# Attention 2's row maxima taken from PSUM three banks at a time in two sets, in place of two banks at a time in three sets

## The chip, the cores and the metric

The kernel runs on one core of one Trainium2 chip. The metric is the device time of one execution in microseconds (us), median of three runs. Below, PE is TensorE (PEld its weight loads), DVE is VectorE, ACT is ScalarE, POOL is GpSimd, SP is SyncE, and SPq is SP's issuing of DMAs.

## What is computed

For each of 16 batches, 512 query rows of 256 channels attend twice to a context of 1601 rows, with a Mamba-2 block between. Attention 2, which the change touches, has 8 heads of 32 channels:

```python
x = _L0_xattn_ref(x, ctx, ctx, mask, ...)          # attention 1, 16 heads of 16, layernorm
h = _mamba2_block(x, ...)
# attention 2
q = (_ln(h, ln_w, ln_b) @ Wq).reshape(b, Lq, 8, 32)
k = (enc @ Wk).reshape(b, Lk, 8, 32)
scores = einsum('bqhd,bkhd->bhqk', q, k) * 1/sqrt(32)
p = softmax(where(pad_mask, -1e9, scores), axis=-1)  # needs the maximum of each row of scores
out = h + (einsum('bhqk,bkhd->bqhd', p, v).reshape(b, Lq, D) @ Wo)
```

## The kernel before

One loop runs over the 16 batches, and each engine has its own program in it, written out by hand and tied to the others by semaphores. An engine executes its program in order, so whatever an engine waits for holds up all that stands behind it.

**The raw stage.** The softmax is taken on transposed scores (keys on the partitions), so each row's maximum has to be known first, as an extra row of the stacked queries. For that, attention 2's scores are computed once more with the queries on the partitions. This stage stands between the Mamba block and attention 2's scoring groups. It works on 2 groups of 4 heads; a group has 4 heads x 4 query tiles x 4 key chunks of 402 columns, 64 products, and each fills one PSUM bank. `entry1` on PE writes the products of an entry into a set of banks (L991), `entry1` on DVE reduces the set to one maximum per product with one instruction (L1642), and frees it. Before the change an entry has 2 products, there are 32 entries in a group, and three sets (banks 0 and 1, 2 and 3, 4 and 5): PE may fill entry n once DVE has freed entry n - 3 (L984). After a group's last entry `maxima1` on DVE folds the four chunk maxima of each row (L1622) and splits the negated maxima in two parts (L1625, L1627). One entry, "turn", stands after the first four entries of group 1: PE transposes the maxima of group 0 into a set (L987), and DVE copies them to a row (L1637). That makes 65 entries (`NENT1`).

**Forward projections.** Between entries PE also projects the first six items of the next batch (`FRONT`: two of queries, 512 columns, four of keys, about 402 columns each, four matmul passes an item, L933), one after every seventh entry (`FRONT_EVERY = 7`, L1319): after entries 6, 13, 20, 27, 34 and 41. They use banks 6 and 7. ACT takes each item out of PSUM in two instructions (`take`, L1372 and L1375), POOL splits it in parts with three instructions (`parts`, L737, L740, L743), with two pieces of the next mask converted after each item (L712). When the last item's parts are done, SP issues `stack(b + 1, 0)` (L655 to L657): 13 transfers inside SBUF that build the stacked keys `KS[0]` and queries `QS[0]` of the next batch's attention 1 (L550, L553, L556). Behind them in SP's program stand the loads of `maskt`.

**What comes after the stage.** PE waits until all entries are freed (L1323), and goes on with attention 2's first scoring group: `scores` (L1010), `times_v` (L1035), and beside them, slot by slot, raw entries of the next batch's attention 1 (`entry`, L971, from `CUTS`, L429). The very first slot has entry 0, which waits for all 13 transfers of `stack(b + 1, 0)` (L954).

```python
def forward():  ...  project(b + 1, front.pop(0), ...)
for n in range(NENT1):
    entry1(b, n)
    if n % FRONT_EVERY == FRONT_EVERY - 1 and front:
        forward()
```

Of the kernel before, what the change touches and what calls it, by code (L numbers as in the profile page):

```python
# [22 lines left out]
ALU = mybir.AluOpType  # L23
ACT = mybir.ActivationFunctionType
AX = mybir.AxisListType
# [4 lines left out]
GH = 4  # L30
# [15 lines left out]
MROW1 = KROWS1 + NPART  # L46
# [5 lines left out]
def xattn_mamba(nc, x, xt, ctxt, mask, maskt, mask1, wq0, bq0, wk0, bk0, wv0, bv0, wo0, bo0, ln_g, ln_b,  # L52
# [4 lines left out]
    QT = T // P  # L57
# [6 lines left out]
    CW = -(-SE // (2 * NCHUNK)) * 2  # L64
# [6 lines left out]
    RAW = GH * QT * NC  # L71
    NENT = G0 * (RAW + 1) + NC + 1
    NCOUNT = G0 * (RAW + 1)
    UNITS = GH * QT * NC // 2
    NENT1 = G1 * UNITS + 1
    NPJ0 = DT + NC + NC + KT
    NPJ = 2 * NPJ0
# [12 lines left out]
    with ExitStack() as ctx:  # L90
# [144 lines left out]

        top = max(top_attention, place[0])
        assert top <= nc.sbuf_usable_end, (top, nc.sbuf_usable_end)

        mask1_s = PR[:, :, :, :].rearrange("p a h t -> p (a h t)").bitcast(U8)[:, 0:S]

# [207 lines left out]
        ENTRIES1 = [("raw", 0, k) for k in range(UNITS)]  # L448
        ENTRIES1 += [("raw", 1, k) for k in range(4)] + [("turn", 0, 0)]
        ENTRIES1 += [("raw", 1, k) for k in range(4, UNITS)]  # L450
        NSETS = 3
        assert len(ENTRIES1) == NENT1

        def raw1_place(k):
            h, i, c = k // (QT * NC // 2), k // (NC // 2) % QT, k % (NC // 2)
            return h, i, c, (PAIRED[2 * c], PAIRED[2 * c + 1])

        OUT_BANK = [5, 7, 6, 3]
        XT1_BANK = [2, 4]
# [442 lines left out]
        def _(pe):  # L902
# [71 lines left out]
            def entry1(b, n):  # L974

                kind, g, k = ENTRIES1[n]
                bank = 2 * (n % NSETS)
                if kind == "raw" and k == 0:
                    for half in range(2):
                        pe.wait_ge(s_k1[g][half], LEAD + (b + 1) * STACK1)  # L980
                    pe.wait_ge(s_k1pad, G1 * (b + 2))
                    pe.wait_ge(s_qs1[g], LEAD + (b + 1) * STACKQ1)
                if n >= NSETS:
                    pe.wait_ge(s_r1free, LEAD + b * NENT1 + n - NSETS + 1)  # L984
                if kind == "turn":
                    pe.wait_ge(s_nm1, b * G1 + g + 1)
                    pe.transpose(ps[0:NPART1 * 16, bank, 0:P], f(nm1[:, :]), ident[:, :]).then_inc(s_r1, 1)  # L987
                    return
                h, i, _, cc = raw1_place(k)
                for e in range(2):  # L990
                    mm = pe.matmul(ps[:, bank + e, 0:CW], QS1[g][0:MROW1 + 1, h, i * P:(i + 1) * P],  # L991
                                   KS1[g][0:MROW1 + 1, h, cc[e]:cc[e] + CW], start=True, stop=True)
                mm.then_inc(s_r1, 1)

            def scores(b, gi, t, between):
# [529 lines left out]
        def _(dve):  # L1525
# [92 lines left out]
            def maxima1(b, g, n):  # L1618

                m = b * G1 + g  # L1620
                dve.wait_ge(s_r1free, LEAD + b * NENT1 + n + 1)
                nc.vector.tensor_reduce(mxr[:, :], mx[:, :, :].rearrange("p c n -> p n c"), AX.X, ALU.max)\  # L1622
                    .then_inc(s_mx1, 1)
                dve.wait_ge(s_mx1, 2 * m + 1)
                nc.vector.tensor_scalar(nm1[:, 0:16], mxr[:, :], -1.0, None, ALU.mult).then_inc(s_mx1, 1)  # L1625
                dve.wait_ge(s_mx1, 2 * m + 2)
                nc.vector.scalar_tensor_tensor(out=nm1[:, 16:32], in0=mxr[:, :], scalar=-1.0, in1=f(nm1[:, 0:16]),  # L1627
                                               op0=ALU.mult, op1=ALU.subtract).then_inc(s_nm1, 1)

            def entry1(b, n):  # L1630

                kind, g, k = ENTRIES1[n]
                bank = 2 * (n % NSETS)
                dve.wait_ge(s_r1, b * NENT1 + n + 1)
                if kind == "turn":
                    dve.wait_ge(s_mload1[1], LEAD + b * 16 * NPART1)
# [1 line left out]
                    dve.wait_ge(s_mrow1, b * G1 + g + 1)  # L1638
                    nc.vector.memset(small[:, 1:2], 0.0).then_inc(s_r1free, 1)
                    return  # L1640
                h, i, c, _ = raw1_place(k)
                nc.vector.tensor_reduce(mx[:, 2 * c:2 * c + 2, h * QT + i], ps[:, bank:bank + 2, 0:CW], AX.X, ALU.max)\  # L1642
                    .then_inc(s_r1free, 1)
                if k == UNITS - 1:
                    maxima1(b, g, n)
# [275 lines left out]
```

## Time and profile before

| | us |
|---|---|
| median of 3 runs | 8576.49 (8573.46 to 8576.82) |
| the profiled execution | 8574.72 |
| its span, first to last instruction | 8572.7 |
| PE busy | 7618.3 (89%) |
| DVE busy | 5016.2 (59%) |
| ACT busy | 3401.1 (40%) |
| POOL busy | 1911.0 (22%) |

A batch takes some 522 us, of which the raw stage is about 63. In the rows of a timeline the columns are start, duration of the merged run of instructions (both us), engine, line, operation, tiles, count, and in brackets the idle time of that engine before it with what ended it. In a table of stretches each engine has its busy us and its count of instructions; PEclk is the clock granted to TensorE (1.00 is 2.4 GHz, 0.50 is 1.2 GHz), DMA the busy share of the 16 DMA engines.

### The profile page before, as it was taken

What the parts mean: (1) busy time and instruction counts of PE and PEld (TensorE: products, weight loads), DVE (VectorE), ACT (ScalarE), POOL (GpSimd) and SP (SyncE); (2) the same over time, 40 slices, a digit from 0 to 9 for tenths busy, and PEclk for the clock granted to TensorE, in tenths of its full rate; (3) what the DMA queues carried; (4) which work ended last, traced back from release to release, by engine and by line L of the source; (5) the groups of instructions that cost most, each with busy time, mean ns of one, the idle gap of its engine ahead of it and who ended that gap; (6) DMA issues with size and microseconds to landing.
All of it is one profiled execution on the core that took longest, in us unless ns stands there. A gap on an engine that the chain in (4) does not pass through costs nothing.

```text
span 8572.7 us, 128046 instructions
## 1 busy us (share of the span) xinstructions
PE 7618.3 (89%) x37252; PEld 3425.4 (40%) x37572; DVE 5016.2 (59%) x12397; ACT 3401.1 (40%) x4278; POOL 1911.0 (22%) x1864
## 2 busy tenths in 40 slices
PE   3989899898998989989899898989989899898998
PEld 0343433434344343433534334343443434335343
DVE  3566465664656556565664656646566565656656
ACT  0424435343352434535244352443524345252443
POOL 3040130402203031130401304022040311304113
PEclk6989989899998989989899898999989999898998
DMA  3142230423314133231422304233141332314223
GB/s 72 27 80 38 41 67 11 80 38 51 58 22 75 30 62 56 36 54 29 77 41 36 66 16 80 38 49 60 20 77 30 59 58 34 56 30 73 45 36 62
DMA packets 230652, 422.16 MB, mean 49 GB/s; under 512 B 37209, under 2 KB 128251, under 8 KB 229769
## 3 DMA queue, kind: packets, MB, share of 16 engines
q1 hardware_dynamic: 227927, 413.21, 28.3%
q8 instruction: 351, 5.75, 0.3%
q14 instruction: 326, 2.67, 0.1%
q10 hardware_dynamic: 2048, 0.53, 0.0%
HBM read 191.17 MB, written 8.54 MB: 23 GB/s over the span
## 4 chain that ended last, share of the span: by engine, by line
PE 73%; DVE 10%; issue 8%; DMA 3%; ACT 3%; SPq 2%; POOL 1%; DVEq 0%; ACTq 0%; POOLq 0%
PE ps L1035 13%; PE ps L971 11%; PE ps L1006 8%; PE ps L933 8%; PE ps L1008 7%; DVE mx L1642 5%; PE ps L1010 4%; PE ps L1040 4%; PE ps L991 2%; PE ps L1191 2%; PE ps L1154 2%; PE ps L1245 1%; DMA qst<-q1hl 1%; PE ps L1273 1%; PE ps L1106 1%
## 5 line engine op out<-in xcount | busy, mean ns | idle before, releaser
L1413 ACT ACTIVATE PR<-ps 128x1024 f32<-128x1024 f32 x2496 | 2498.3, 1023 | 2514.8 <-PE ps L1008 1395.2
L1613 DVE CUSTOM_DVE_ANT_0 ps<-ps,maskq 128x402 f32<-128x402 f32 x4203 | 2408.7, 587 | 1517.2 <-PE ps L971 1374.8
L1035 PE MATMUL ps<-PR,vbuf 128*32 128x512 f32 x9984 | 1346.9, 612 | 5.1 <-ACT PR L1413 5.1
L1008 PE MATMUL ps<-maskk,identb 128*128 128x512 bf16 x3008 | 1142.8, 380 | 0.0
L971 PE MATMUL ps<-kst,qst 96*128 96x402 bf16 (+1 forms) x3115 | 1017.9, 340 | 97.0 <-DVE mx L1613 67.8
L1642 DVE TENSOR_REDUCE mx<-ps 128x2 f32<-128x804 f32 x1024 | 933.6, 985 | 197.6 <-PE ps L991 195.6
L991 PE MATMUL ps<-kst,qst 100*128 100x402 f32 x2048 | 751.5, 494 | 257.9 <-DMA qst<-q1hl 155.2
L1006 PE MATMUL ps<-qst,kst 99*128 99x512 bf16 x2496 | 950.9, 381 | 7.3
L1010 PE MATMUL ps<-qst,kst 102*128 102x512 f32 x1664 | 768.0, 526 | 100.1 <-ACT PR L1413 70.7
L971 PEld LDWEIGHTS ps<-kst,qst 96*128 96x128 bf16 x3115 | 282.1, 97 | 1183.9 <-DVE mx L1613 817.5
L751 POOL MEMSET kst<- 96x252 f32 (+1 forms) x34 | 8.7, 255 | 3061.8 <-PE ps L1035 3015.4
L991 PEld LDWEIGHTS ps<-kst,qst 100*128 100x128 f32 x2048 | 416.7, 241 | 571.5 <-DVE mx L1642 381.9
L1613 DVE DVE_READ_ACCUMULATOR2_ANT mx<- 128x1 f32 x4203 | 591.6, 141 | 0.0
L1651 DVE RECIPROCAL rsm<-ps 128x128 f32<-128x128 f32 x80 | 76.6, 957 | 866.3 <-PE ps L1059 866.3
L712 POOL TENSOR_SCALAR maskk<-stage 128x512 bf16<-128x512 int32 (+1 forms) x238 | 428.3, 1800 | 336.6 <-DMA stage<-in_maskt 328.6
L971 PE MATMUL ps<-KS,QS 96*128 96x402 bf16 x1088 | 410.8, 378 | 102.9 <-DVE mx L1613 74.1
L712 POOL TENSOR_SCALAR maskq<-stage 128x402 bf16<-128x402 int32 (+1 forms) x272 | 427.4, 1571 | 301.7 <-DMA stage<-in_mask 278.9
L933 PE MATMUL ps<-ctxs,wk_s 128*128 128x402 f32 (+1 forms) x1056 | 468.5, 571 | 24.0 <-ACT rest L1375 23.1
L1040 PE MATMUL ps<-PR,ones 128*32 128x512 f32 x3328 | 447.8, 610 | 0.0
L1008 PEld LDWEIGHTS ps<-maskk,identb 128*128 128x128 bf16 x3328 | 327.3, 98 | 265.4 <-issue 1.3
L1010 PEld LDWEIGHTS ps<-qst,kst 102*128 102x128 f32 x1664 | 330.1, 206 | 244.5 <-ACT PR L1413 151.0
L1006 PEld LDWEIGHTS ps<-qst,kst 99*128 99x128 bf16 x2496 | 243.9, 98 | 410.2 <-ACT PR L1413 183.9
(197 smaller groups left out, 7899.2 us busy)
## 6 DMA issues: line engine op xcount, KB each, us to landing
kst<-khl SPq DMA_DIRECT2D x300, 200.1 KB, 7.7
stage<-in_maskt SPq DMA_DIRECT2D x204, 256.0 KB
stage<-in_mask SPq DMA_DIRECT2D x204, 201.0 KB
kst<-khl SPq DMA_DIRECT2D x96, 402.0 KB, 8.6
kst<-khl SPq DMA_DIRECT2D x96, 398.5 KB, 11.6
ctxs<-in_ctxt SPq DMA_DIRECT2D x17, 1601.0 KB, 17.7
qst<-q1hl SPq DMA_DIRECT2D x96, 256.0 KB
win_s<-in_w_in SPq DMA_DIRECT2D x16, 1288.0 KB, 5.7
```

The costliest lines, as they stand in the source:

```text
L712: nc.gpsimd.tensor_scalar(dst, stage[0:rows, n % 2, 0:w], 0.0, MASKED, ALU.is_equal, ALU.mult)\
L933: mm = pe.matmul(o, l, r, start=(k == 0), stop=(k == DT - 1))
L971: pe.matmul(ps[:, bank, 0:w], QS[gi][0:KROWS, h, i * P:(i + 1) * P], KS[gi][0:KROWS, h, c0:c0 + w], start=True, stop=True).then_inc(s_raw, 1)
L991: mm = pe.matmul(ps[:, bank + e, 0:CW], QS1[g][0:MROW1 + 1, h, i * P:(i + 1) * P], KS1[g][0:MROW1 + 1, h, cc[e]:cc[e] + CW], start=True, s ...
L1006: pe.matmul(o, KS[gi][0:SROWS, h, t * P:(t + 1) * P], QS[gi][0:SROWS, h, :], start=True, stop=False)
L1008: mm = pe.matmul(o, identb[:, :], maskk[:, t, :], start=False, stop=True)
L1010: mm = pe.matmul(o, KS1[gi - G0][0:SROWS1, h, t * P:(t + 1) * P], QS1[gi - G0][0:SROWS1, h, :], start=True, stop=True)
L1035: mm = pe.matmul(ps[32 * j:32 * j + 32, 6, :], l, PR[:, t % 2, j, :], start=(t == 0), stop=(t == KT - 1), tile_position=(0, 32 * j))
L1040: mm = pe.matmul(ps[32 * j:32 * j + 32, 7, :], ones[:, 0:32], PR[:, t % 2, j, :], start=(t == 0), stop=(t == KT - 1), tile_position=(0, 32 ...
L1413: nc.scalar.activation(PR[:, t % 2, 2 * half:2 * half + 2, :], ps[:, 2 * half:2 * half + 2, :], ACT.Exp, scale=scale).then_inc(s_p, 1)
L1613: nc.vector.tensor_tensor_reduce(src, src, maskq[:, i, c0:c0 + w], 1.0, -3.0e38, ALU.add, ALU.max, mx[:, c, h * QT + i:h * QT + i + 1]).th ...
L1642: nc.vector.tensor_reduce(mx[:, 2 * c:2 * c + 2, h * QT + i], ps[:, bank:bank + 2, 0:CW], AX.X, ALU.max)\
```

## The change

An entry now has three products in place of two (`WIDE = 3`), so a group has 22 entries: 21 of three banks and one of a single bank, since 64 is 21 x 3 + 1. There are two sets (banks 0 to 2 and 3 to 5) in place of three: PE may fill entry n once DVE has freed entry n - 2. The stage has 45 entries in place of 65. The products are numbered through, so the maxima are stored in another order, and the reduction of `maxima1` reads them accordingly. The number of products, the columns of each, the turn after the first four entries of group 1, and `FRONT_EVERY` are as they were.

```diff
-    UNITS = GH * QT * NC // 2
+    WIDE = 3
+    UNITS = -(-GH * QT * NC // WIDE)
...
+        mx_flat = mx[:, :, :].rearrange("p c n -> p (c n)")
...
-        NSETS = 3
+        NSETS = 2
-        def raw1_place(k):
-            h, i, c = k // (QT * NC // 2), k // (NC // 2) % QT, k % (NC // 2)
-            return h, i, c, (PAIRED[2 * c], PAIRED[2 * c + 1])
+        def raw1_chunks(k):
+            return range(WIDE * k, min(WIDE * (k + 1), GH * QT * NC))
...
-                bank = 2 * (n % NSETS)
+                bank = WIDE * (n % NSETS)
...
-                h, i, _, cc = raw1_place(k)
-                for e in range(2):
+                for e, n in enumerate(raw1_chunks(k)):
+                    h, i, c = n // (QT * NC), n // NC % QT, n % NC
                     mm = pe.matmul(ps[:, bank + e, 0:CW], QS1[g][0:MROW1 + 1, h, i * P:(i + 1) * P],
-                                   KS1[g][0:MROW1 + 1, h, cc[e]:cc[e] + CW], start=True, stop=True)
+                                   KS1[g][0:MROW1 + 1, h, PAIRED[c]:PAIRED[c] + CW], start=True, stop=True)
...
-                nc.vector.tensor_reduce(mxr[:, :], mx[:, :, :].rearrange("p c n -> p n c"), AX.X, ALU.max)\
+                nc.vector.tensor_reduce(mxr[:, :], mx_flat.rearrange("p (n c) -> p n c", c=NC), AX.X, ALU.max)\
...
-                h, i, c, _ = raw1_place(k)
-                nc.vector.tensor_reduce(mx[:, 2 * c:2 * c + 2, h * QT + i], ps[:, bank:bank + 2, 0:CW], AX.X, ALU.max)\
+                done = raw1_chunks(k)
+                nc.vector.tensor_reduce(mx_flat[:, done[0]:done[-1] + 1], ps[:, bank:bank + len(done), 0:CW], AX.X, ALU.max)\
```

## Rows read from the trace of the kernel before

**Rows 1.** The page: the chain that ended last, by engine.

```profile
PE 73%; DVE 10%; issue 8%; DMA 3%; ACT 3%; SPq 2%; POOL 1%; DVEq 0%; ACTq 0%; POOLq 0%
```

**Rows 2.** Groups of instructions, whole run: count, busy us, mean ns, idle before, releaser.

```profile
L1642 DVE TENSOR_REDUCE mx<-ps 128x2 f32<-128x804 f32 x1024 | 933.6, 985 | 197.6 <-PE ps L991 195.6
...
L1559 DVE TENSOR_TENSOR vbuf<-ps,bv_s 128x256 f32<-128x256 f32 (+1 forms) x208 | 88.2, 424 | 43.0 <-PE ps L933 26.5
```

**Rows 3.** Timeline of DVE, first batch's raw stage.

```profile
551.29 6.41 DVE L1642 TENSOR_REDUCE mx<-ps 128x2 f32<-128x804 f32 x7 [9.07 <-PE ps L991]
559.80 12.92 DVE L1642 TENSOR_REDUCE mx<-ps 128x2 f32<-128x804 f32 x14 [2.10 <-PE ps L991]
573.78 10.01 DVE L1642 TENSOR_REDUCE mx<-ps 128x2 f32<-128x804 f32 x11 [1.06 <-PE ps L991]
583.82 0.26 DVE L1622 TENSOR_REDUCE mxr<-mx 128x16 f32<-128x64 f32 x1
584.42 2.79 DVE L1642 TENSOR_REDUCE mx<-ps 128x2 f32<-128x804 f32 x3
...
588.40 0.27 DVE L1637 CAST mrow_f<-ps 32x128 fp32r<-32x128 f32 x1
...
588.80 25.35 DVE L1642 TENSOR_REDUCE mx<-ps 128x2 f32<-128x804 f32 x28
```

**Rows 4.** Timeline of PE, same stage: fills alone.

```profile
550.21 2.38 PE L991 MATMUL ps<-kst,qst 100*128 100x402 f32 x6 [9.71 <-DMA qst<-q1hl]
...
588.54 0.99 PE L991 MATMUL ps<-kst,qst 100*128 100x402 f32 x4 [0.61 <-DVE mx L1642]
...
595.26 0.63 PE L991 MATMUL ps<-kst,qst 100*128 100x402 f32 x2 [0.26 <-DVE mx L1642]
```

**Rows 5.** Timeline of PE, same stage: four of the six forward projections.

```profile
555.88 3.51 PE L933 MATMUL ps<-ctxn,wq_s 128*128 128x512 f32 x4
...
564.02 1.88 PE L933 MATMUL ps<-ctxn,wq_s 128*128 128x512 f32 x4
...
584.68 2.40 PE L933 MATMUL ps<-ctxs,wk_s 128*128 128x402 f32 x4
...
591.23 1.49 PE L933 MATMUL ps<-ctxs,wk_s 128*128 128x395 f32 x4
```

**Rows 6.** Table of stretches by granted clock (columns: PE, PEld, DVE, ACT, POOL, PEclk, DMA).

```profile
549.00:559.10 10.10, 8.89 (x19) 5.52 (x19) 6.41 (x7) 0.00 (x0) 2.01 (x2) 0.50 0.80 108
559.20:569.40 10.20, 8.17 (x30) 4.82 (x29) 9.49 (x11) 2.53 (x4) 8.85 (x8) 1.00 0.29 80
569.50:572.80 3.30, 3.26 (x7) 1.84 (x6) 3.21 (x4) 0.00 (x0) 3.14 (x3) 0.50 0.02 4
572.90:583.00 10.10, 8.15 (x31) 4.74 (x29) 9.22 (x11) 2.17 (x4) 8.49 (x9) 1.00 0.30 82
583.20:586.40 3.20, 3.20 (x7) 2.01 (x7) 3.10 (x7) 0.00 (x0) 3.04 (x3) 0.50 0.03 6
586.60:596.60 10.00, 8.01 (x31) 4.69 (x29) 9.65 (x13) 2.15 (x4) 7.59 (x9) 1.00 0.29 79
596.80:614.00 17.20, 15.47 (x34) 8.53 (x34) 17.20 (x20) 0.00 (x0) 3.34 (x3) 0.50 0.89 129
```

**Rows 7.** Timelines of ACT, POOL and SPq behind the last forward projection.

```profile
592.76 0.59 ACT L1372 ACTIVATE khl<-ps,cols 128x395 bf16<-128x395 f32 x1 [4.56 <-PE ps L933]
...
594.38 0.88 POOL L737 TENSOR_TENSOR rest<-rest,khl 128x395 f32<-128x395 f32 x1
...
596.06 0.94 POOL L743 TENSOR_TENSOR khl<-rest,khl 128x395 bf16<-128x395 f32 x1
...
597.46 4.77 SPq L553 DMA_DIRECT2D KS<-khl  x6
602.28 5.32 SPq L556 DMA_DIRECT2D QS<-qhl  x6
```

**Rows 8.** Table of stretches at the stage's end, columns as in rows 6.

```profile
612.00:613.00 1.00, 0.53 (x2) 0.00 (x0) 1.00 (x2) 0.00 (x0) 0.00 (x0) 0.50 0.97 320
613.00:614.00 1.00, 0.00 (x0) 0.00 (x0) 1.00 (x2) 0.00 (x0) 0.00 (x0) 0.50 0.12 41
```

**Rows 9.** Timeline of PE at the start of the first scoring group.

```profile
614.37 0.79 PE L1010 MATMUL ps<-qst,kst 102*128 102x512 f32 x1 [1.84 <-DVE mx L1642]
614.96 0.56 PE L971 MATMUL ps<-KS,QS 96*128 96x402 bf16 x1
```

More of the change, by code:

```diff
@@ L1632, in entry1 @@
                 kind, g, k = ENTRIES1[n]
-                bank = 2 * (n % NSETS)
+                bank = WIDE * (n % NSETS)
                 dve.wait_ge(s_r1, b * NENT1 + n + 1)
```

## The prediction

> **What bounds the kernel now.** I read the chain of waits first. It is 73% PE and 10% DVE [rows 1]. The group of L1642 alone has 933.6 us of busy time in the whole run [rows 2], 58 us of each batch's raw stage of 63. So in this stage, and here only, DVE sets the pace. Its timeline shows that: after the turn it does 28 reductions in 25.35 us without an idle moment; less the 0.98 of the last that is 24.37 over 27 steps, 0.90 us each [rows 3]. In its first half it idles 2.10 and 1.06 us, both behind a forward projection on PE [rows 3, 5]. PE meanwhile does a pair of products in 0.63 us and then idles 0.26 [rows 4]. Second, I read the granted clock. It is 1.00 in three stretches of 10 us and 0.50 between them, and stays at 0.50 from 596.8 on, when PE has no more forward projections [rows 6]. Third, I followed what the forward projections are for, since the change shifts them: that chain ends at the transfers of `stack(b + 1, 0)` [rows 7 to 9], and it decides the forecast. I work on the first batch's stage; the other 15 are alike within 3 us. Times below count from PE's first product, at 550.2.
>
> **1. Fewer reductions (a gain).** A reduction of 804 columns takes 0.985 us [rows 2] and DVE starts one every 0.90. What 402 more columns cost is not in the trace. From 256 to 804 columns read from PSUM, in two different operations, 0.424 grows to 0.985 [rows 2], 1.02 ns a column, or 0.41 us for 402; half a step would be 0.45. I take 0.42, so a wide reduction lasts 1.40 and its step is 1.32, or 0.44 us a bank against 0.45. By steps, 42 x 1.32 + 2 x 0.48 = 56.4 us against 64 x 0.90 = 57.7: 1.3 us less in a stage, 21 us in all. With 0.45 for the third bank it is nothing (1.35 a step, 0.45 a bank), and with 0.41 it is 28 us. The fixed part by the rows is 0.90 - 0.84 = 0.06 us for each of the 20 reductions saved.
>
> The Trainium skill, "Perfetto Trace Analysis", section "Optimizing Scalar/DVE Operations", gives DVE about 125 ns of access overhead per operation on PSUM and says that grouping into larger operations improves throughput if the engine is saturated. By that figure the 20 reductions would be worth 2.5 us a stage, 40 us in all; the trace shows half of it. The same section says that breaking up instructions may let work be completed sooner where DVE causes bubbles on other engines, and that speaks against this change.
>
> **2. Two sets in place of three (a loss at the low clock).** With two sets, a set's cycle is its reduction plus its refill, and two cycles interleave. Refill of two banks at the high clock: 0.63 us; four banks 0.99, so 0.18 a bank and 0.81 for three. At the low clock six banks took 2.38 us [rows 4]; a bank is 402 columns at 1.2 GHz, 0.335, so three take 1.37. Some 0.05 us of handover lies on either side. High: 1.40 + 0.81 + 0.10 = 2.31 for two steps, under 2 x 1.32, so DVE stays the bound. Low: 1.40 + 1.37 + 0.10 = 2.87 against 2.64, 0.11 us lost an entry. Before, three sets had 2.7 us for 0.98 + 1.04 + 0.10, so nothing was lost. With 40 entries, half to all of them low: 2 to 4.5 us a stage; none if the clock stays high.
>
> **3. Less cover for a forward projection (a loss).** Count from the moment that a set comes free. High clock: PE's streams of three banks end after 0.05 + 0.10 + 0.55 = 0.70; a key item takes 1.34 (the last took 1.49 with its tail, [rows 5]); the next set is filled 0.76 later, at 2.8. DVE has the rest of one reduction (1.24) and one more (1.32), until 2.56: it idles 0.25. For a query item (1.71) 0.6. Low clock: streams end at 1.2, a key item takes 2.68, the next set is full at 5.1, and DVE ran out at 2.78: it idles 2.4; for a query item (3.41) 3.1. The same recipe for the kernel before gives 0 and 0.2 at high, 1.85 and 2.6 at low; the trace has 2.10 after the first (low, with the clock rising during it) and 1.06 after the third, which ran partly low [rows 3, 5, 6].
>
> **4. The projections meet the low clock.** Before, six projections are one in 7 x 0.90 = 6.3 us plus stalls. One that runs at the low clock is followed by 10 us of high clock, and the next one falls into it: the pattern of low, high, low, high [rows 5, 6]. After, they are 7 x 1.32 = 9.3 us apart plus 2 of stalls, so most of them start when the clock has fallen again. I count, for projections 1 to 5, idle times on DVE of 2.2 (low, clock rising), 3.1, then 1.2, 2.4 and 2.1: 11 us, against 3.4 for the same five before (2.10 and 1.06 by the trace, 0.2 by the recipe). Bounds: all at the high clock 2 x 0.6 + 3 x 0.25 = 2.0; all at the low one 2 x 3.1 + 3 x 2.4 = 13.4.
>
> **5. maxima1, the short entry, the turn.** `maxima1` takes DVE 0.6 (583.82 to 584.42 [rows 3]), as before, and covers the refill behind the one-bank entry at the high clock. The turn takes 0.4 (588.40 to 588.80), in which the set behind it can't be refilled in time: 0.6 (high) to 1.1 (low) us of idle.
>
> **6. When the last forward projection ends.** This is the term that matters. Before, it is the sixth of 65 entries' worth, after entry 41, and ends at 592.7, 42.5 us into the stage; 23 entries follow. After, entry 41 is one of 45, and three follow. First reduction starts at 1.4. Entries 0 to 39, which have to be reduced before entry 41 can be filled, are 38 wide ones, a short one and the turn: 38 x 1.32 + 0.48 + 0.6 + 0.4 = 51.7. Then 0.7 to 1.2 of filling and the item itself, 1.34 to 2.68, likely 2.3. With stalls of 11, bubbles of 2 and the turn's 1.1: 1.4 + 51.7 + 1.0 + 2.3 + 14.1 = 70.5. Since some of these stalls overlap a bubble already counted, I take 69.5. Bounds: all high 1.4 + 51.7 + 0.7 + 1.3 + 2.0 + 0.6 = 57.7; all low 1.4 + 51.7 + 1.2 + 2.7 + 13.4 + 1.1 + 4.4 = 75.9.
>
> **7. What hangs on it.** Behind the last item stand ACT (592.76), POOL (594.38 to 597.0), then twelve DMA issues on SP's queue from 597.46 to 607.6 [rows 7], and the transfers keep the DMA engines at 0.97 until 613, when the share drops to 0.12 [rows 8]. That is 20.3 us from the end of the item. Before, 20.7 us of reductions covered it, and the transfers landed 2 us before PE first needs them: L971 starts at 614.96, 64.8 us into the stage, released by the end of the stage, not by a DMA [rows 9]. After the change only three entries, 3 us, stand there. The chain is as long (0.5 shorter, as POOL will not be busy with a mask piece when the item comes), so L971 can start at 69.5 + 19.8 = 89.3, which is 24.5 us later than before. PE is in order, and L971 is its second matmul of the scoring group, so all of attention 2's scoring and the raw entries of the next batch beside it wait, about 14 us in which PE, ACT and DVE have nothing. The stage itself gets some 10 us longer, which ends inside this wait. The `maskt` loads behind the transfers shift with them and with the scoring group, and the two rows of maxima that ACT issues behind the last `take` come before the transfers land; both cost nothing more. PE starts the scoring group at the low clock as it does now.
>
> **Sum.** 16 x 24.5 = 392 us on a span of 8572.7. The profiled run took 8574.7 and the median is 8576.5, so I add it to the median: 8968, and say 8970. Bounds by step 6: all high 57.7 + 19.8 - 64.8 = 12.7 a batch, 203 in all, 8780; all low 75.9 + 19.8 - 64.8 = 30.9, 494, 9070.
>
> **The rivals.**
> - The stage alone grows (10%): the transfers turn out to be hidden, because they run faster once nothing competes, or because PE finds other work first. Then the cost is steps 1 to 5: about 11 - 3.4 + 2 + 0.5 - 1.3 = 9 us a batch, 144 in all, 8720. Against it: L954 stands in the first slot, and the 10 us of issues on SP's queue [rows 7] don't depend on load.
> - The wait is there, but the clock stays high (10%): 8780 to 8880. For it: the clock's fall depends on how busy PE is, and the trace has only this pace. Against it: PE is less busy per us after the change.
> - The clock stays low throughout (8%): 9040 to 9070.
> - Faster (4%): DVE's 1.3 us a batch are all that counts, 8555. It needs both that every refill is shorter than the other set's reduction, so the high clock throughout (2.31 under 2.64), and that the last forward projection has its 20 us of cover elsewhere. It decides at a third bank of under 0.45 us. The chain of step 7 speaks against the second half.
> - The change doesn't do what it says (3%): the wide reduction runs slower per column than 1.05 ns. A nanosecond a column more is 1.2 us a reduction and 50 us a stage; anything above 0.2 would show.
>
> The Trainium skill, "TensorE: Matmul & The Clock Gate", section "A second HAM failure mode: psum-queue depth-cycling", describes a kernel in which short idle times between groups of matmuls that cycle through PSUM banks made the clock alternate between its two levels. The trace agrees: in this stage the clock alternates [rows 6]. It is the rule behind the rival of the low clock.
>
> **How the numbers follow.** The forecast has 65%, between 8910 and 9030. The range of 8 in 10 leaves out the rivals under 8840: 8840 to 9050. A measurement of this kernel tells about 0.2% from no change, 17 us. Faster by more has 4%, within it 2%, slower 94%.
>
> **What would show it.** In the profile after: L1642 with 1402 ns for 1206 columns; DVE idle 1.2 to 3 us behind every forward projection; the last L933 of the stage three entries before its end, about 69 us in; and PE idle 12 to 16 us before the first L971, ended by the DMA QS<-qhl. If that wait is missing, step 7 is wrong; if it is there but of 5 us or 25, step 4 is.

## The result and the profile after

| | before | after |
|---|---|---|
| median of 5 runs, us | 8576.49 (8568.29 to 8581.33) | 9033.92 (9018.61 to 9048.93) |
| ratio, with 95% interval | | 1.0535 (1.0524 to 1.0547) |
| the profiled execution; its span, us | 8574.72; 8572.7 | 9048.93; 9047.2 |
| PE / DVE busy, us | 7618.3 / 5016.2 | 7715.3 / 5022.8 |
| mean granted clock of TensorE | 0.924 | 0.899 |

The kernel is 457 us slower; 393 were forecast. The profiled execution is the longest of the five, so the two spans differ by 474.5 us, and the accounts below are of that difference. In the kernel after, the raw stage's products are L993 (before L991), its reductions L1644 (L1642), the forward projections L935 (L933), the next batch's raw entries L973 (L971), and the scoring group's first product L1012 (L1010).

First two groups of instructions of the whole run (busy us, mean ns, then idle before them with its releasers), then the reductions with their shapes kept apart:

```profile
L973 PE MATMUL ps<-KS,QS 96*128 96x402 bf16 x1088 | 410.1, 377 | 345.7 <-DMA QS<-qhl 261.1 <-DVE mx L1615 80.9
...
L1644 DVE TENSOR_REDUCE mx<-ps 128x3 f32<-128x1206 f32 x704 | 931.4, 1370 | 383.2 <-PE ps L993 363.8
```

By shape:

```profile
L1644 DVE TENSOR_REDUCE mx<-ps 128x3 f32<-128x1206 f32 x672 | 914.5, 1408 | 363.3 <-PE ps L993 343.8
L1644 DVE TENSOR_REDUCE mx<-ps 128x1 f32<-128x402 f32 x32 | 18.3, 572 | 20.0 <-PE ps L993 20.0
```

The group of L971 in the kernel before was

```profile
L971 PE MATMUL ps<-KS,QS 96*128 96x402 bf16 x1088 | 410.8, 378 | 102.9 <-DVE mx L1613 74.1 <-DMA QS<-qhl 23.5
```

Two sums stand out. PE's idle time before the next batch's raw entries has grown by 242.8 us, 15.2 a batch, and transfers into `QS` now end it. DVE's idle time before its reductions has grown by 185.6 us (383.2 against 197.6, [rows 2]), 11.6 a batch. The reductions' busy time fell by 2.2 us only.

DVE's timeline of the first batch's stage, whose first product starts at 551.50, answers to [rows 3] (start, duration of the merged run, idle before):

```profile
552.90 10.05 DVE L1644 TENSOR_REDUCE mx<-ps 128x3 f32<-128x1206 f32 x7 [9.38 <-PE ps L993]
565.83 9.82 DVE L1644 TENSOR_REDUCE mx<-ps 128x3 f32<-128x1206 f32 x7 [2.87 <-PE ps L993]
577.33 9.58 DVE L1644 TENSOR_REDUCE mx<-ps 128x3 f32<-128x1206 f32 x7 [1.68 <-PE ps L993]
588.51 0.58 DVE L1644 TENSOR_REDUCE mx<-ps 128x1 f32<-128x402 f32 x1 [1.60 <-PE ps L993]
...
597.38 1.41 DVE L1644 TENSOR_REDUCE mx<-ps 128x3 f32<-128x1206 f32 x1 [1.15 <-PE ps L993]
600.48 9.58 DVE L1644 TENSOR_REDUCE mx<-ps 128x3 f32<-128x1206 f32 x7 [1.69 <-PE ps L993]
612.33 9.61 DVE L1644 TENSOR_REDUCE mx<-ps 128x3 f32<-128x1206 f32 x7 [2.27 <-PE ps L993]
623.95 3.22 DVE L1644 TENSOR_REDUCE mx<-ps 128x3 f32<-128x1206 f32 x3 [2.01 <-PE ps L993]
```

Every seven entries DVE has nothing for 1.6 to 2.9 us. Where [rows 3] show 14 and 28 reductions in one piece, none here is longer than seven. PE's timeline of the same stage shows two entries at the low clock, one at the high clock, and the six forward projections, which answer to [rows 4, 5]; then the start of the scoring group, which answers to [rows 9]:

```profile
554.38 2.69 PE L993 MATMUL ps<-kst,qst 100*128 100x402 f32 x6 [0.50 <-DVE mx L1644]
...
561.30 3.62 PE L935 MATMUL ps<-ctxn,wq_s 128*128 128x512 f32 x4
...
574.00 2.75 PE L935 MATMUL ps<-ctxn,wq_s 128*128 128x512 f32 x4
...
585.25 2.88 PE L935 MATMUL ps<-ctxs,wk_s 128*128 128x402 f32 x4
...
597.13 2.76 PE L935 MATMUL ps<-ctxs,wk_s 128*128 128x402 f32 x4
...
604.59 0.82 PE L993 MATMUL ps<-kst,qst 100*128 100x402 f32 x3 [0.50 <-DVE mx L1644]
...
608.40 2.88 PE L935 MATMUL ps<-ctxs,wk_s 128*128 128x402 f32 x4
...
620.28 2.84 PE L935 MATMUL ps<-ctxs,wk_s 128*128 128x395 f32 x4
...
627.40 0.79 PE L1012 MATMUL ps<-qst,kst 102*128 102x512 f32 x1 [1.52 <-DVE mx L1644]
642.76 0.49 PE L973 MATMUL ps<-KS,QS 96*128 96x402 bf16 x1 [14.57 <-DMA QS<-qhl]
```

The key projections of 402 columns take 2.76 to 2.88 us, and none takes the 1.49 of [rows 5]. The table of stretches says why (columns as in [rows 6]: PE, PEld, DVE, ACT, POOL, granted clock, DMA share). Its last row is the long wait:

```profile
585.20:588.40 3.20, 3.20 (x7) 1.86 (x7) 1.71 (x2) 0.22 (x1) 0.00 (x0) 0.50 0.25 66
596.70:600.00 3.30, 3.30 (x8) 2.04 (x8) 1.41 (x1) 0.07 (x1) 0.00 (x0) 0.55 0.16 55
625.00:642.70 17.70, 1.24 (x2) 0.47 (x2) 2.74 (x6) 0.00 (x0) 4.86 (x5) 0.56 0.84 119
```

From 625 to 642.7 PE works 1.24 us, DVE 2.74 and ACT nothing, while the DMA engines are at 0.84. What lies between the last projection (ends 623.12) and L973 is seen on ACT, POOL and SPq, as in [rows 7]:

```profile
623.16 0.59 ACT L1374 ACTIVATE khl<-ps,cols 128x395 bf16<-128x395 f32 x1 [10.75 <-PE ps L935]
...
626.06 0.94 POOL L745 TENSOR_TENSOR khl<-rest,khl 128x395 bf16<-128x395 f32 x1
...
627.45 4.85 SPq L555 DMA_DIRECT2D KS<-khl  x6
632.36 5.27 SPq L558 DMA_DIRECT2D QS<-qhl  x6
```

Issuing the twelve transfers takes SP's queue until 637.63; PE's entry starts 5.1 us after that. In all it is 19.6 us from the projection's end to L973, where step 7 had 19.8.

**The same over all 16 batches.** Means in us from each stage's first product, read off the timelines; low clock is the time at 0.50 in the stretch named:

| | before | after |
|---|---|---|
| last forward projection ends | 42.3 | 71.6 |
| stage ends | 63.7 | 75.8 |
| last transfer of the stack landed | 62.5 | 91.2 |
| first L971 / L973 | 64.5 | 91.4 |
| from there to the next stage | 457.0 | 459.7 |
| low clock in the stage | 31.9 | 47.1 |
| low clock from first L971 / L973 to the next stage | 37.4 | 41.7 |

So 26.9 us of each batch's loss lie up to L973 (430 in all) and 2.7 behind it (43 in all): together 473, and the spans differ by 474.5.

### The profile page after: what moved, and what is told of

Read it like the earlier page. It is cut to its first block, busy times and chain, and to the rows that moved or that the text cites. A ratio compares the mean times of both kernels' runs of the same rounds, so it can differ in the third digit from the quotient of the medians.

```text
span 9047.2 us, 127102 instructions
## 1 busy us (share of the span) xinstructions
PE 7715.3 (85%) x37252; PEld 3529.8 (39%) x37572; DVE 5022.8 (56%) x12077; ACT 3403.2 (38%) x4278; POOL 1913.4 (21%) x1864
## 4 chain that ended last, share of the span: by engine, by line
PE 73%; DVE 10%; issue 6%; DMA 4%; SPq 3%; ACT 3%; POOL 1%; DVEq 0%; ACTq 0%; POOLq 0%
PE ps L1037 13%; PE ps L973 11%; PE ps L935 9%; PE ps L1008 8%; PE ps L1010 7%; DVE mx L1644 5%; PE ps L993 3%; PE ps L1012 3%; PE ps L1042 3%; PE ps L1193 2%; PE ps L1156 2%; PE ps L1247 1%; SPq L555 1%; DMA qst<-q1hl 1%; PE ps L1275 1%
## 5 line engine op out<-in xcount | busy, mean ns | idle before, releaser
L1415 ACT ACTIVATE PR<-ps 128x1024 f32<-128x1024 f32 x2496 | 2499.6, 1024 | 2504.2 <-PE ps L1010 1417.5
L1010 PE MATMUL ps<-maskk,identb 128*128 128x512 bf16 x3008 | 1147.0, 381 | 0.0
L1644 DVE TENSOR_REDUCE mx<-ps 128x3 f32<-128x1206 f32 x704 | 931.4, 1370 | 383.2 <-PE ps L993 363.8
L973 PE MATMUL ps<-kst,qst 96*128 96x402 bf16 (+1 forms) x3115 | 1024.0, 342 | 93.6 <-DVE mx L1615 65.6
L993 PE MATMUL ps<-kst,qst 100*128 100x402 f32 x2048 | 764.4, 506 | 378.3 <-DVE mx L1644 219.2
L1008 PE MATMUL ps<-qst,kst 99*128 99x512 bf16 x2496 | 950.6, 381 | 7.3
L1012 PE MATMUL ps<-qst,kst 102*128 102x512 f32 x1664 | 767.2, 524 | 95.3 <-ACT PR L1415 70.9
L973 PEld LDWEIGHTS ps<-kst,qst 96*128 96x128 bf16 x3115 | 282.9, 97 | 1181.7 <-DVE mx L1615 812.8
L993 PEld LDWEIGHTS ps<-kst,qst 100*128 100x128 f32 x2048 | 482.6, 260 | 646.0 <-DVE mx L1644 441.3
L973 PE MATMUL ps<-KS,QS 96*128 96x402 bf16 x1088 | 410.1, 377 | 345.7 <-DMA QS<-qhl 261.1
L935 PE MATMUL ps<-ctxs,wk_s 128*128 128x402 f32 (+1 forms) x1056 | 521.1, 626 | 25.5 <-ACT rest L1377 24.5
L1374 ACT ACTIVATE khl<-ps,cols 128x402 bf16<-128x402 f32 (+1 forms) x136 | 81.0, 596 | 1121.6 <-PE ps L935 1121.6
L973 PEld LDWEIGHTS ps<-KS,QS 96*128 96x128 bf16 x1088 | 110.1, 101 | 852.7 <-DVE mx L1615 478.9
L1010 PEld LDWEIGHTS ps<-maskk,identb 128*128 128x128 bf16 x3328 | 328.0, 99 | 267.3 <-issue 4.0
```

Source lines behind the costliest of these rows:

```text
L935: mm = pe.matmul(o, l, r, start=(k == 0), stop=(k == DT - 1))
L973: pe.matmul(ps[:, bank, 0:w], QS[gi][0:KROWS, h, i * P:(i + 1) * P], KS[gi][0:KROWS, h, c0:c0 + w], start=True, stop=True).then_inc(s_raw, 1)
L1008: pe.matmul(o, KS[gi][0:SROWS, h, t * P:(t + 1) * P], QS[gi][0:SROWS, h, :], start=True, stop=False)
L1010: mm = pe.matmul(o, identb[:, :], maskk[:, t, :], start=False, stop=True)
L1012: mm = pe.matmul(o, KS1[gi - G0][0:SROWS1, h, t * P:(t + 1) * P], QS1[gi - G0][0:SROWS1, h, :], start=True, stop=True)
L1415: nc.scalar.activation(PR[:, t % 2, 2 * half:2 * half + 2, :], ps[:, 2 * half:2 * half + 2, :], ACT.Exp, scale=scale).then_inc(s_p, 1)
```

## The experiments

The theory: the changed kernel loses its time because the last forward projection, one after every seventh entry, now stands three entries before the stage's end, and the chain of transfers behind it is uncovered. It ends as late as it does in part for its place and in part for the stalls that two sets can't cover at the low clock. The rivals: the stage's own length is the loss and the transfers are incidental; or the wide reduction is what costs. Each run has the runs of the kernel before made beside it; ratios are against those, with medians from 8574.0 to 8574.8.

**1. The changed kernel with a forward projection after every fifth entry**

```diff
-        FRONT_EVERY = 7
+        FRONT_EVERY = 5
```

> The changed kernel with one forward projection after every fifth entry in place of every seventh (after entries 4, 9, 14, 19, 24 and 29 of 45), nothing else. Theory (the late last projection is what costs most): the last one ends about 48 us into the stage in place of 71.6, the transfers behind it land at 68, inside the stage, and the wait of 14.6 us before the first L973 is gone. L973 then starts when the stage ends, at 66 to 72 us in place of 91.3: 16 x (91.3 - 69) = 357 us less than the changed kernel's 9034, so 8680 (8640 to 8730), still 1% above the kernel before, because of the thinner cover (two sets) that remains. Rival (the three-bank sets themselves cost the 457 us, wherever the projections stand): 8950 or more, and the wait stays.

Measured 8724.4 (8714.3 to 8726.0), ratio 1.0170 (1.0153 to 1.0187). From the kernel after, 310 of 457 us are back. The group of L973 and one stall of DVE's timeline:

```profile
L973 PE MATMUL ps<-KS,QS 96*128 96x402 bf16 x1088 | 411.0, 378 | 109.6 <-DVE mx L1615 81.2 <-DMA QS<-qhl 24.5
```

The stall behind the second projection:

```profile
572.58 6.94 DVE L1644 TENSOR_REDUCE mx<-ps 128x3 f32<-128x1206 f32 x5 [2.94 <-PE ps L993]
```

L973 idles 109.6 us, as before the change (102.9). The last projection ends 51.4 us into the stage, the transfers land at 71.0, L973 starts at 73.0. What is left, 150 us, is the stage itself, 72.2 us against 63.7 (times 16 is 136), and a rest of the batch that is 0.9 us longer. The wait on the transfers is thus the larger part of the loss, and it hangs on where the last projection stands. The stage alone can't be the loss.

**2. The kernel before, with the projections moved late**

```diff
-        FRONT_EVERY = 7
+        FRONT_EVERY = 10
```

> The kernel before, pairs and three sets, with one forward projection after every tenth entry (after 9, 19, ... 59 of 65), nothing else. It delays the last projection alone. Theory: it ends at 63 to 65 us, only 5 entries before the end; the transfers land 19.8 us later, at 83 to 85; L971 starts there and not at 64.5, with 14 to 18 us of PE idle before it, ended by the DMA QS<-qhl. 16 x 20 = 320, so 8895 us (8850 to 8940). Rival (transfers hidden, only stalls of projections that meet the low clock): the stage grows by some 5 us, 8576 + 80 = 8656.

Measured 8887.0, ratio 1.0364 (1.0343 to 1.0385). Pairs and three sets are untouched, and the long wait is there. PE at the start of the scoring group, and the group over the whole run:

```profile
622.58 0.79 PE L1010 MATMUL ps<-qst,kst 102*128 102x512 f32 x1 [2.24 <-DVE mx L1642]
636.50 0.50 PE L971 MATMUL ps<-KS,QS 96*128 96x402 bf16 x1 [13.13 <-DMA QS<-qhl]
```

The group:

```profile
L971 PE MATMUL ps<-KS,QS 96*128 96x402 bf16 x1088 | 409.6, 377 | 323.9 <-DMA QS<-qhl 244.1 <-DVE mx L1613 74.3
```

The last projection ends at 64.7, the transfers land at 84.3: the chain is 19.6 us again. Wide reductions aren't needed for the wait; lateness is enough.

**3. The kernel before, with two sets of pairs**

```diff
-        NSETS = 3
+        NSETS = 2
```

> The kernel before with two sets of two banks in place of three (FRONT_EVERY stays 7, 65 entries), nothing else. It takes the depth away and leaves the width. Theory (each set less is cover lost: at the low clock 0.98 + 1.04 + 0.10 = 2.12 for two steps of 0.90, and behind a projection only 1.7 us of cover): a stage of 74 to 81 us in place of 63.8, the last projection at 54, its transfers at 74, just hidden. 16 x 14 = 224, so 8800 us (8750 to 8850). Rival (depth does not matter as DVE is the bound): 8576 to 8590.

Measured 8823.5, ratio 1.0290 (1.0269 to 1.0310). The stage grew to 79.5 us, and the last projection ended at 54.8, early enough that the group of L971 idled 104.0 us, no more than before. DVE late in the stage, at the low clock:

```profile
614.14 1.90 DVE L1642 TENSOR_REDUCE mx<-ps 128x2 f32<-128x804 f32 x2 [0.23 <-PE ps L991]
616.26 1.90 DVE L1642 TENSOR_REDUCE mx<-ps 128x2 f32<-128x804 f32 x2 [0.23 <-PE ps L991]
```

The group of all reductions:

```profile
L1642 DVE TENSOR_REDUCE mx<-ps 128x2 f32<-128x804 f32 x1024 | 967.6, 991 | 417.1 <-PE ps L991 413.2
```

Two entries take 2.13 us. Step 2's rule (a set's cycle is its reduction, its refill and 0.10) gives 0.98 + 1.04 + 0.10 = 2.12. So going from three sets to two makes the stage longer by itself, at the same width. Three banks in a set are better than two in that respect: two sets of pairs have a stage of 79.5 us, two sets of three banks with about the same distance in banks between projections (15 against 14) 72.2.

**4. The kernel before, with the projections moved early**

```diff
-        FRONT_EVERY = 7
+        FRONT_EVERY = 5
```

> The kernel before with one forward projection after every fifth entry (after 4, 9, 14, 19, 24 and 29 of 65), nothing else. Theory (a projection that starts at the high clock is covered by three sets, and projections close together keep the clock high): stalls behind projections fall from 4 us to 1 or 2, the stage goes from 63.8 to 61 us, and the transfers, earlier by 13 us, stay hidden: 8576 - 16 x 2.8 = 8532 us (8515 to 8560). Rival (POOL, which needs 6.2 us for each item with its two mask pieces, holds the projections up at a spacing of 4.5 us, and DVE starves behind them): 8576 or more.

Measured 8578.9 (10 runs), ratio 1.0005 (0.9995 to 1.0014), no difference, where 0.5% less was expected. Its stage did get shorter, 61.9 us against 63.7, and the idle time before the reductions fell:

```profile
L1642 DVE TENSOR_REDUCE mx<-ps 128x2 f32<-128x804 f32 x1024 | 930.9, 984 | 168.1 <-PE ps L991 166.1
```

But from its first L971 to the next stage a batch now takes 459.4 us, 2.4 more, and of these 43.4 are at the low clock, where it was 37.4. The gain of the stage is given back in the rest of the batch, in which no instruction was changed.

**5. PE kept busy to the stage's end.** The kernel before with a projection after every fifth entry, and each product of an entry past 30 computed twice:

```diff
-        FRONT_EVERY = 7
+        FRONT_EVERY = 5
...
-                for e in range(2):
+                for e in (0, 1, 0, 1) if n > 30 else (0, 1):
```

> The kernel before with one forward projection after every fifth entry, and with each product of entries 31 to 64 computed twice into the same bank, so that PE is kept busier behind the last projection; nothing else, and the result of a product is the same. Theory (the clock falls behind the last projection because PE has little to do there; at the high clock a pair done twice takes 1.0 us, hidden behind three sets, and the first scoring group then starts at the high clock in place of 9 us at the low one): granted clock 1.00 at the end of the stage, stage about 61.5 us, the first scoring group 3 to 5 us shorter than with every fifth alone (8579). 16 x 4 = 64, so 8515 us (8490 to 8550). Rival (the clock at the end of the stage does not matter, or four products an entry make PE the bound): 8579 to 8640.

Measured 8567.3 (10 runs), ratio 0.9990 (0.9980 to 0.9999). The expectation of 8515 missed. In the stage the clock did what it was to do. Two stretches of this run, and the start of the scoring group in the kernel before:

```profile
600.00:616.00 16.00, 14.14 (x64) 10.04 (x62) 15.56 (x21) 0.10 (x1) 3.65 (x2) 1.00 0.82 121
616.00:626.00 10.00, 9.48 (x37) 3.00 (x35) 5.83 (x20) 4.30 (x5) 7.80 (x5) 0.66 0.40 114
...
614.00:623.90 9.90, 9.46 (x29) 3.45 (x33) 6.30 (x21) 4.09 (x4) 7.69 (x4) 0.50 0.24 80
```

The stage's end runs at 1.00, where [rows 6] had 0.50. At the start of the scoring group the clock is still low for a part of the time, 0.66 where it was 0.50. But the stage takes 63.6 us, 1.7 more than in run 4: the second products have a price of their own. The batches whose stage has 7.1 us at the low clock need 62.4 us for it, those with 12.3 us need 64.1.

**6. The same with FRONT_EVERY at 7.** The products are computed twice in all entries that don't stand beside a projection:

```diff
-                for e in range(2):
+                for e in (0, 1) if n < 42 and n % 7 in (0, 6) else (0, 1, 0, 1):
```

> The kernel before, FRONT_EVERY 7 as it was, with each product computed twice in all entries except the ones next to a forward projection (n % 7 of 0 and 6 up to entry 41). Theory (the clock is the second cause: a projection that meets the low clock costs 1 to 2 us of idle DVE, one at the high clock at most 0.2): the granted clock stays at 1.00 after its first rise, stalls fall from 3.4 to about 1.5 us, stage 61 in place of 63.7, and the scoring group starts at the high clock, 4 us more: 8576 - 16 x 6 = 8480 us (8460 to 8530). Rival (more work on PE only lengthens the fills): stage of 64 or more, 8580 or more.

Measured 8562.7 (10 runs), ratio 0.9985 (0.9976 to 0.9995). The sign is right, the size is an eighth (12 us for 95). The stage before the change spends 31.9 us at the low clock, this one 5.2, and DVE's idle time fell from 197.6 to 169.7 us: that is 1.7 us a stage. Directly behind the stage the clock is low again for a part, as in run 5:

```profile
600.00:610.00 10.00, 10.00 (x46) 7.34 (x44) 10.00 (x13) 0.00 (x0) 0.00 (x0) 1.00 1.07 134
612.00:622.00 10.00, 8.99 (x34) 3.16 (x35) 7.03 (x21) 4.09 (x4) 7.73 (x5) 0.66 0.34 90
```

With three sets of pairs the low clock costs the stage little, since DVE sets the pace. Runs 5 and 6 price the clock for the kernel before only together with the second products: a gain of 0.1 and 0.15%, both intervals just clear of no change. That the stalls of the changed kernel need both, the low clock and the lack of cover, rests on step 2's rule and on one stage of run 9.

**7. The other way: single banks in six sets.** The changed kernel's code with one product an entry; the turn and the projections stand behind the same products as before the change:

```diff
-    WIDE = 3
+    WIDE = 1
...
-        NSETS = 2
+        NSETS = 6
...
-        FRONT_EVERY = 7
+        FRONT_EVERY = 14
```

> The changed kernel with one product an entry and six sets of one bank (129 entries, a forward projection after every 14th, the turn after eight entries), so the same six banks and the same projections beside the same products as in the kernel before. Theory (the fixed part of a reduction is 0.06 us, and finer sets cover more: 5 banks ahead in place of 4): 128 x 0.48 = 61.8 us of reductions and less idle behind projections, stage 64 to 66 us, the last projection at 42, its transfers hidden: 8576 + 16 x 1.3 = 8597 us (8575 to 8640). Rival (the count of reductions counts more than their cover, as the change assumes): each extra reduction costs 0.12 or more, 64 x 0.12 = 8 us a stage, 8700.

Measured 8602.6 (8601.5 to 8604.9), ratio 1.0032 (1.0019 to 1.0046).

```profile
L1644 DVE TENSOR_REDUCE mx<-ps 128x1 f32<-128x402 f32 x2048 | 998.7, 568 | 174.5 <-PE ps L993 174.4
```

Twice as many reductions add 65.1 us of busy time to DVE (998.7 against 933.6), 0.064 us for each of the 1024 more, and idle time falls by 23.1; the kernel is 28 us slower. Halving the grouping and deepening the sets costs 0.3%; the step to more grouping and fewer sets cost 5.35%, of which 1.7% are left when the projections are spaced anew (run 1).

**8. The changed kernel with the first entries of the next batch later.** This leaves the stage alone and takes the scoring group's need for the transfers away from its first three key tiles:

```diff
-        CUTS = [(0, 61, 0, KT - 1)], ...
+        CUTS = [(0, 61, 3, KT - 1)], ...
```

> The changed kernel, FRONT_EVERY 7, with the 61 raw entries beside the first scoring group spread over its key tiles 3 to 12 and not 0 to 12, nothing else. Theory (what stands still is only PE's program behind L973, which waits for the transfers; scoring itself needs none of them): PE does three key tiles, 9 us or more of work, before it reaches the first L973, so the wait of 14.6 us shrinks to 3 to 6; some of that is given back, as 61 entries of 0.79 us on DVE then share ten tiles. 9034 - 16 x 8 = 8906 us (8850 to 8970). Rival (the scoring group waits for the transfers or their traffic in another way): 9030 and the same wait.

Measured 8974.0, ratio 1.0465 (1.0444 to 1.0486), 60 us less than the kernel after and 68 more than expected. PE at the start of the scoring group, and the group:

```profile
642.88 0.83 PE L973 MATMUL ps<-KS,QS 96*128 96x402 bf16 x2 [4.56 <-DMA QS<-qhl]
```

The group:

```profile
L973 PE MATMUL ps<-KS,QS 96*128 96x402 bf16 x1088 | 398.6, 370 | 187.7 <-DMA QS<-qhl 94.9 <-DVE mx L1615 80.1
```

The transfers land when they did (91.2 us into the stage), while the idle time that they end fell from 261.1 to 94.9 us, 10.4 a batch. Only 4 us a batch reached the end. The rest went into the scoring group, where the 61 entries now stand beside ten key tiles in place of thirteen; which of its waits took it was not worked out. Here, filling the wait with other work of the same batch brought 60 us, and moving what it waits for (run 1) 310.

**9. Run 1 with PE kept busy.** As run 1, and each entry's first product is computed twice:

```diff
-                for e, n in enumerate(raw1_chunks(k)):
+                chunks = list(enumerate(raw1_chunks(k)))
+                for e, n in chunks[:1] + chunks:
```

> The changed kernel with a forward projection after every fifth entry, and with the first product of each entry computed twice into its bank (four matmuls an entry in place of three), nothing else. It keeps PE busier, at the price of 0.19 us of filling an entry at the high clock, 0.34 at the low one. Theory (the stalls of 2.3 to 2.9 us behind each projection are so long because the projections meet the low clock; at the high clock they are 0.6 to 1.0): once risen, the clock stays at 1.00 from about 11 to 45 us of the stage, the stalls behind projections 2 to 5 fall to 1 us or less, and the stage goes from 72 to 69 or 70 us although more work is done: 8724 - 16 x 2.5 = 8685 us (8650 to 8720). Rival (two sets are too few at either clock, so the stalls stay and the filling comes on top): stage of 75 us or more, 8770.

Measured 8751.7 (8750.0 to 8756.6), ratio 1.0208 (1.0191 to 1.0225): 27 us slower than run 1, where 40 less was expected. DVE's timeline (the reduction is L1645 here) and two stretches:

```profile
563.68 6.70 DVE L1645 TENSOR_REDUCE mx<-ps 128x3 f32<-128x1206 f32 x5 [2.31 <-PE ps L994]
571.30 6.70 DVE L1645 TENSOR_REDUCE mx<-ps 128x3 f32<-128x1206 f32 x5 [0.92 <-PE ps L994]
578.55 5.38 DVE L1645 TENSOR_REDUCE mx<-ps 128x3 f32<-128x1206 f32 x4 [0.55 <-PE ps L994]
```

The stretches:

```profile
570.00:580.00 10.00, 7.85 (x34) 5.67 (x32) 8.53 (x8) 2.35 (x4) 7.89 (x7) 1.00 0.26 66
605.00:620.00 15.00, 14.66 (x39) 10.76 (x40) 13.46 (x10) 0.00 (x0) 3.47 (x3) 0.56 0.92 128
```

Where the clock is 1.00 the stall behind a projection is 0.92 and 0.55 us, where run 1 has 2.94 and 2.27 at the same two: step 3's split between the clocks is seen in one stage. But late in the stage the clock is at 0.56 all the same, and there the extra product costs 0.2 us an entry. Over all batches the low clock in the stage fell from 42.1 to 36.1 us, and the stage still grew from 72.2 to 74.9: the filler held the clock up for a part of the stage only, and cost more than that gave.

## Why the prediction was right

The direction and the mechanism held, and the time of 9033.9 lies 64 us above the forecast, inside the range. By its steps:

**Step 1, fewer reductions: the price was right, the gain was not had.** Forecast 1.40 us for a wide reduction and 1.32 from one to the next; the rows have 1.408, and two reductions in a row start 1.32 apart. The fixed part by the rows was 0.06 us, and run 7 gives 0.064. The Trainium skill, "Perfetto Trace Analysis", section "Optimizing Scalar/DVE Operations", puts it at about 125 ns; the trace has half of that. Its sentence in the same place, that breaking instructions up may be better where DVE causes bubbles elsewhere, is tested by no run alone. Run 7 is 431 us faster than the kernel after, but it also has the projections back beside their old products, and it is 28 us slower than the kernel before. Of the 21 us forecast, only 2.2 show in the busy time. A reduction that waited for its set doesn't overlap with the one before it, and loses the 0.08 us between 1.40 and 1.32; that happens at every stall and bubble.

**Step 2, two sets: right.** At the low clock 2.87 was forecast for two entries; PE's runs of two start at 554.38 and 557.25, 2.87 apart. At the high clock fills start 1.32 apart, DVE's own pace. Run 3 has the same rule with pairs, 2.13 measured for 2.12.

**Steps 3 and 4, the stalls: right in sum, not one by one.** Forecast 2.2, 3.1, 1.2, 2.4 and 2.1 us behind projections 1 to 5, 11.0 in all; measured 2.87, 1.68, 1.60, 1.69 and 2.27, 10.1 in all. All six projections began at the low clock, where step 4 had most of them do so; the clock rose behind them, and the stalls lie between the prices of step 3 for the two clocks (0.6 and 3.1 for queries, 0.25 and 2.4 for keys). That the sum fits within 1 us is luck in part: the second was put 1.4 too high, the first 0.7 too low. The stage grew by 12.1 us (75.8 against 63.7), where step 7 had some 10.

**Steps 5 and 6, the end of the last projection: 2 us too early.** Forecast 69.5, measured 71.6, as mean and in the first batch. The working had 70.5 and took 1.0 off, for stalls counted twice. That was a choice with no row behind it, and it was wrong. The rest in the first batch: stalls and the turn together 0.8 less than counted and bubbles 0.2 more; the short entry with `maxima1` behind it 0.6 more (from 589.09, its reduction's end, to 590.31, where 0.6 was counted); the 0.08 us of overlap lost at seven breaks, 0.6; the item itself 2.84 and not 2.3. In each of 16 batches 2.1 us are 34 us. Not all of the lateness is stalls: the item ends 29.3 us later than before the change, and by step 6's sum with the high clock throughout (57.7 against 42.3) some 15 of these come from its place behind 42 wider entries, which is an estimate.

**Step 7, the chain: right.** 19.8 us forecast, 19.8 as the mean from the projection's end to L973, of which 10.2 are the issues on SP's queue. The wait on PE was to be 12 to 16 us and is 14.57 in the first batch and 15.2 as the growth of the group's idle time per batch. Runs 1 and 2 show the cause from both sides: with the projections earlier the wait is gone in the changed kernel, with the projections later it is there in the kernel before.

**The term that was missing: the rest of the batch.** The sum took the time from L973 to the next stage as unchanged, and it grew by 2.7 us, 43 in all. With the 34 us of step 6 that makes 77 of the 82 by which the forecast of 392 fell short of 474.5; 4 more are L971 of the kernel before, which the sum took from the first batch (64.8) where the mean is 64.5. No instruction was changed in the rest of the batch, but two things in it changed.

One is a wait. At the end of the loop's body PE jumps back to the loop's head, and its first product there is L1006 (L1008 after). The groups of these products over the run, the jumps on PE's sequencer (PEldq; ns min/median/max), and the place behind the third pass through the loop, each before and after:

```profile
L1006 PE MATMUL ps<-QS,KS 99*128 99x512 bf16 x832 | 318.4, 383 | 32.2 <-issue 32.2
L1008 PE MATMUL ps<-QS,KS 99*128 99x512 bf16 x832 | 322.3, 387 | 46.6 <-issue 46.6
...
L1127 PEldq COMPARE_BRANCH  x16: 83/3470/3790, 743.9 to 8567.3; - x16
L1129 PEldq COMPARE_BRANCH  x16: 83/4334/5277, 774.2 to 9041.6; - x16
...
1792.54 0.38 PE L1006 MATMUL ps<-QS,KS 99*128 99x512 bf16 x1 [1.92 <-issue]
1879.25 0.38 PE L1008 MATMUL ps<-QS,KS 99*128 99x512 bf16 x1 [3.91 <-issue]
```

The 83 ns are the last jump, which isn't taken. PE idles 14.4 us more at the loop's head over the run. In eight of the 15 batches it idles 3.5 to 4.1 us, where the kernel before has 2.4 at most, and in each of these eight the low clock follows directly. They take 461.2 us on average from L973 to the next stage, the other seven 458.0.

The other thing is where the low clock falls. After that wait the kernel after has the first of these stretches, 136 us into its scoring, and the kernel before, at the same place in its work, the second (columns as in [rows 6]):

```profile
1879.00:1883.00 4.00, 3.66 (x10) 1.57 (x12) 1.50 (x5) 1.02 (x1) 0.00 (x0) 0.58 0.57 177
```

The kernel before:

```profile
1792.30:1796.30 4.00, 3.29 (x15) 1.85 (x17) 2.22 (x7) 1.75 (x2) 0.00 (x0) 1.00 0.17 51
```

PE is no less busy and does two thirds of the matmuls. Over the kernels the length of the rest goes with the low clock in it and with that wait (us; run 8 is left out, as its first L973 stands later in the program):

| | low clock, a batch | PE idle at the loop's head, whole run | from first L971 / L973 to the next stage, a batch |
|---|---|---|---|
| run 2 | 33.8 | 31.0 | 455.9 |
| run 7 | 35.2 | 33.4 | 456.2 |
| run 9 | 35.4 | 32.2 | 456.8 |
| run 6 | 35.6 | 33.6 | 456.5 |
| run 5 | 36.1 | 33.5 | 457.3 |
| run 3 | 36.3 | 31.6 | 456.2 |
| before | 37.4 | 32.2 | 457.0 |
| run 1 | 37.9 | 41.3 | 457.9 |
| after | 41.7 | 46.6 | 459.7 |
| run 4 | 43.4 | 31.3 | 459.4 |

Run 4 has the longer rest without the longer wait. That the length goes with the low clock, and in the kernel after and run 1 with the wait too, is shown. Why the jump takes longer in the kernel after, and what in the stage decides where the later low stretches fall, is not: no run moved either at will, and both stay open.

**The rivals.** The stage alone: it was to be 8720, with 9 us more a stage, and the kernel after has 12.1 more and the wait on top. Run 1, where the wait is gone, has 8724; that this is the rival's number is luck in part, as its projections stand elsewhere and its stage grew by 8.4 us only. The high clock throughout: ruled out by the six projections of 2.75 to 3.62 us. The low clock throughout: the time came near its 9040, but for other reasons; L993 has 604.59 with 0.82 us for three banks, which is the high clock. A slower wide reduction: 1.408 us rules it out.

## What to carry to other kernels

Before grouping instructions over a fixed number of PSUM banks, compare the draining time of the banks that are filled ahead with the longest work put between two fills, at the low clock: the ungrouped form cost 0.3% here, the grouped form with fewer sets 1.7% with the projections moved forward and 5.35% without. Work placed after every n-th entry moves when an entry changes size, and what counts is the chain behind the last such item: 20 us of it had 20.7 us of cover, and the change left 3. A change that shifts the clock in one stage is to be measured over the whole period, the untouched part too, since here a stage's gain of 1.8 us came back as 2.4 us elsewhere.

## What the runs showed of the hardware

- **A higher clock alone was worth little where another engine set the pace.** In run 6 the stage spent 5.2 us at the low clock in place of 31.9, and the kernel gained 0.15%, the price of the second products included.
- **A busy PE did not always get the high clock.** At the stage's end before the change PE was busy for 15.47 of 17.20 us with the clock at 0.50 [rows 6]; in run 9 it was busy for 14.66 of 15 us at 0.56, and the clock stayed low to the stage's end.
- **An edit in one stage moves the low clock in stages that are the same.** Between the ten kernels above it was 33.8 to 43.4 us a batch in the unchanged rest, which took 455.9 to 459.7 us.
- **The jump back to the loop's head had no fixed price here.** On PE it took 3.3 to 3.8 us in the 15 passes before the change and up to 5.3 after (L1127, L1129), and PE idled 1.9 to 4.1 us meanwhile.
- **Reductions from PSUM back to back overlap.** One of 402, 804 or 1206 columns takes 0.57, 0.98 or 1.41 us, and the next starts after 0.49, 0.90 or 1.32: about 0.08 us is had only if the next set is already full.
